# First attention's scores: two f32r products of stacked high and low parts in place of one f32 product

## What is computed

```python
h = h + _L0_attn_ref(_layernorm(h, axis=-1), L0_attn_Wq, L0_attn_bq, L0_attn_Wk, L0_attn_bk, L0_attn_Wv, L0_attn_bv)
...
q = jnp.einsum('bnh,oh->bno', x, Wq) + bq
k = jnp.einsum('bnh,oh->bno', x, Wk) + bk
v = jnp.einsum('bnh,oh->bno', x, Wv) + bv
scores = jnp.einsum('bik,bjk->bij', q, k)
attention = jax.nn.softmax(scores, axis=-1)
attended = jnp.einsum('bij,bjk->bik', attention, v)
```

## Time and profile before

| what | value |
|---|---|
| median of 3 runs | 5632.31 us (5630.87 to 5649.04) |
| the profiled execution | 5644.55 us |
| its span, first to last instruction | 5642.7 us |
| TensorE (PE) busy | 4372.6 us, 77% |
| VectorE busy | 3331.4 us, 59% |
| ScalarE busy | 1815.6 us, 32% |
| GpSimd busy | 425.7 us, 8% |
| TensorE on the chain that ended last | 49% of the span |
| mean granted TensorE clock | 0.822 |

### The profile page before, as it was taken

How to read it: one execution, slowest core, us unless ns; L and a number is a source line. 1 busy time by engine, 2 the same in 40 slices (tenths; PEclk the granted TensorE clock), 3 DMA queues, 4 the chain that set the end, 5 groups by cost and what they waited for, 6 DMA issues and landing times.

```text
span 5642.7 us, 71238 instructions
## 1 busy us (share of the span) xinstructions
PE 4372.6 (77%) x26536; PEld 2924.2 (52%) x26536; DVE 3331.4 (59%) x9075; ACT 1815.6 (32%) x2723; POOL 425.7 (8%) x484
## 2 busy tenths in 40 slices
PE   6886755799888755699888755699887765699987
PEld 4554544555646534555546534555546544555646
DVE  4444769555545669555555669555555659655554
ACT  2232521144332522134332422134332421234432
POOL 0100000011100000011100000021100000011100
PEclk9898865699988975599988975699988975689988
DMA  2000000000000000000000000000000000000000
GB/s 80 3 3 15 1 16 1 1 1 1 1 1 4 1 16 1 1 1 1 1 1 4 1 16 1 1 1 1 1 1 4 1 1 1 1 1 1 1 1 4
DMA packets 28309, 26.48 MB, mean 5 GB/s; under 512 B 10550, under 2 KB 26934, under 8 KB 27450
## 3 DMA queue, kind: packets, MB, share of 16 engines
q1 hardware_dynamic: 27962, 21.98, 1.4%
HBM read 20.40 MB, written 1.57 MB: 4 GB/s over the span
## 4 chain that ended last, share of the span: by engine, by line
PE 49%; DVE 29%; issue 5%; POOL 4%; ACT 3%; DVEq 1%; SPq 0%; POOLq 0%; ACTq 0%
PE ps L581 10%; PE ps L615 7%; DVE qup L759 4%; PE ps L1584 3%; DVE x L757 3%; PE ps L1600 3%; DVE x L761 3%; DVE ctxt L802 3%; PE ps L642 3%; DVE ctxt L798 2%; POOL st L394 2%; PE ps L915 2%; PE ps L414 2%; PE ps L427 2%; DVE row_max L1047 2%
## 5 line engine op out<-in xcount | busy, mean ns | idle before, releaser
L615 PE MATMUL ps<-cst,big 128*128 128x128 f32 x4608 | 674.9, 298 | 345.0 <-ACT big L717 312.5
L615 PEld LDWEIGHTS ps<-cst,big 128*128 128x128 f32 x4608 | 570.1, 154 | 426.3 <-ACT big L717 354.9
L698 ACT COPY big<-ps 128x512 f32<-128x512 f32 x816 | 478.6, 586 | 877.1 <-PE ps L615 877.1
L832 DVE TENSOR_REDUCE negmax<-ps 128x1 f32<-128x1536 f32 x336 | 590.1, 1757 | 64.0 <-PE ps L588 44.8
L717 ACT ACTIVATE big<-ps,negmax 128x1536 f32<-128x1536 f32 x336 | 518.7, 1544 | 269.0 <-DVE negmax L832 269.0
L409 PE MATMUL ps<-cst 128*128 128x512 f32 x608 | 332.5, 707 | 127.4 <-DVEq L187 58.2
L394 POOL TENSOR_TENSOR st<-st,cst 128x6 f32<-128x6 f32 x104 | 156.8, 1508 | 3449.3 <-DVE st L382 3445.2
L581 PE MATMUL ps<-kup,qup 128*128 128x512 f32 (+3 forms) x768 | 358.1, 563 | 41.8 <-POOLq L187 41.0
L588 PE MATMUL ps<-qlo 128*128 128x512 f32 x576 | 343.9, 736 | 7.4 <-DVEq L187 7.4
L422 ACT COPY xt<-ps 64x512 f32<-64x512 f32 x144 | 80.7, 579 | 828.0 <-PE ps L414 828.0
L642 PE MATMUL ps<-big,v 128*32 128x128 f32 (+1 forms) x8064 | 324.7, 278 | 8.1 <-DVE ctxt L1071 6.0
(11 more groups left out here) (317 smaller groups left out, 7131.4 us busy)
## 6 DMA issues: line engine op xcount, KB each, us to landing
rw<-in_w_route SPq DMA_DIRECT2D x128, 64.5 KB, 1.8
cst<-in_consts SPq DMA_DIRECT2D x1, 2671.0 KB, 14.7
cst<-in_consts SPq DMA_DIRECT2D x1, 2670.5 KB, 8.8
big<-in_consts SPq DMA_DIRECT2D x1, 1872.5 KB, 22.0
out_dram<-res SPq DMA_DIRECT2D x4, 384.0 KB, 2.8
experts_in<-in_consts SPq DMA_DIRECT2D x1, 1360.0 KB, 17.5
qup<-in_patches SPq DMA_DIRECT2D x4, 260.0 KB
klo<-in_pe_low SPq DMA_DIRECT2D x2, 384.0 KB, 23.3
```

The lines of the kernel that those rows point to most:

```text
L615: ins = nc.tensor.transpose(turned_bank(kind, u, g)[:, i * P:(i + 1) * P], prob[:, slot_of(kind, u), (4 * g + i) * P:(4 * g + i + 1) * P], ...
L698: copy(pt[:, slot_of(kind, u), g, 0:n], turned_bank(kind, u, g)[:, 0:n]).then_inc(*ph.mark(copier(kind, g)))
L832: nc.vector.tensor_reduce(negmax[:, u:u + 1], flat[:, 0:n], AX.X, ALU.max, negate=True)\
```

## The change

q and k of the first attention are no longer kept in f32. TensorE makes each of them twice, one copy under the other: the weights are repeated by VectorE at the start of each batch (`twice`), and a product has 128 output rows in place of 64. The blocks come as q, k, q, k, q, k. ScalarE writes each block rounded to f32r (the high part) to `q_stack` or `k_stack`. VectorE then subtracts it from the exact block: in the lower half of the rows of q (64 to 127), so that `q_stack` holds the high part above the low part; for k on all 128 rows into a second plane, so that plane 0 of `k_stack` holds the high part twice and plane 1 the low part twice. The scores of a bank are two f32r products with the same stationary `q_stack` tile, added in PSUM: (q high + q low) with k high, then with k low. POOL no longer clears `qlo` in this phase.

```diff
-        def qkv_pe(ph, pe, wq, wk, wv):
+        def qkv_blocks():
+
+            return [(w, j) for j in range(NB) for w in range(2)]
+
+        def qkv_pe(ph, pe):
             keep_clock(1, 9)
             pe.wait_ge(*ph.after("normed", 1))
             transpose_pe(ph, x, [0, 1, 2])
-            for j in range(NB):
+            pe.wait_ge(*ph.after("weights_spread", 2))
+            for i, (w, j) in enumerate(qkv_blocks()):
                 pe.wait_ge(*ph.after("xt_copied", j + 1))
-                nc.tensor.matmul(ps[0:D, 3 + j, :], W(wq), xt[:, 512 * j:512 * (j + 1)], start=True, stop=True)\
-                    .then_inc(*ph.mark("q_psum"))
-            for j in range(NB):
-                nc.tensor.matmul(ps[0:D, (6 + j) % 8, :], W(wk), xt[:, 512 * j:512 * (j + 1)], start=True, stop=True)\
-                    .then_inc(*ph.mark("k_psum"))
-            rows_pe(ph, W(wv), xt, [1, 2], "v_psum")
+                nc.tensor.matmul(ps[:, (3 + i) % 8, :], twice[:, w, :, :].rearrange("p r d -> p (r d)"), xt[:, 512 * j:512 * (j + 1)], start=True, stop=True)\
+                    .then_inc(*ph.mark("stack_psum"))
+            rows_pe(ph, W("v0"), xt, [1, 2], "v_psum")
...
-            for j in range(NB):
-                act.wait_ge(*ph.after("k_psum", j + 1))
-                nc.scalar.copy(kt[0:D, 512 * j:512 * (j + 1)], ps[0:D, (6 + j) % 8, :])
...
+            for i, (w, j) in enumerate(qkv_blocks()):
+                act.wait_ge(*ph.after("stack_psum", i + 1))
+                nc.scalar.activation((q_stack, k_stack)[w][:, 0, 512 * j:512 * (j + 1)].bitcast(F32R), ps[:, (3 + i) % 8, :],
+                                     ACT.Identity).then_inc(*ph.mark("high_ready"))
...
+        def qkv_vec(ph, dve):
+            for i, (w, j) in enumerate(qkv_blocks()):
+                cols = slice(512 * j, 512 * (j + 1))
+                dve.wait_ge(*ph.after("high_ready", i + 1))
+                if w == 0:
+                    ins = nc.vector.scalar_tensor_tensor(q_stack[D:P, 0, cols].bitcast(F32R), ps[D:P, (3 + i) % 8, :], 1.0,
+                                                         q_stack[D:P, 0, cols], ALU.mult, ALU.subtract)
+                else:
+                    ins = nc.vector.scalar_tensor_tensor(k_stack[:, 1, cols].bitcast(F32R), ps[:, (3 + i) % 8, :], 1.0,
+                                                         k_stack[:, 0, cols], ALU.mult, ALU.subtract)
+                ins.then_inc(*ph.mark("low_ready"))
...
+                elif kind == "attn0":
+                    for part in range(2):
+                        ins = nc.tensor.matmul(bank, q_stack[:, 0, qs].bitcast(F32R), k_stack[:, part, lo * P:hi * P].bitcast(F32R),
+                                               start=(part == 0), stop=(part == 1))
...
                 pool.wait_ge(consts_in, CONST_DMAS)
-                clear_upper(ph, pool)
                 norm_pool(ph, pool, 1)
...
+                for w, name in enumerate(("q0", "k0")):
+                    nc.vector.tensor_copy(twice[:, w, :, :], W(name).unsqueeze(1).to_broadcast([P, 2, D]))\
+                        .then_inc(*ph.mark("weights_spread"))
                 dve.wait_ge(patches_in, 32 * (b + 1))
                 nc.vector.tensor_copy(h[:, TP:T, :], txt_in)
```

More of the change, by code:

```diff
@@ L51 @@
 SIGNALS = {
-    "embed": {"pool_step": 1, "rstd_ready": 2, "xt_copied": 3, "emb_psum": 1, "xt_psum": 3, "q_psum": 3, "k_psum": 3,
+    "embed": {"weights_spread": 2, "rstd_ready": 2, "xt_copied": 3, "emb_psum": 1, "xt_psum": 3, "stack_psum": 6, "high_ready": 6, "low_ready": 6,
         "v_psum": 2, "vec_step": 13, "var_ready": 2, "normed": 1},
@@ L277, in build @@
         work = qup[:, 0, :]
+        twice = big[:, 0:2 * P].rearrange("p (w r d) -> p w r d", w=2, r=2)
         spread = big[:, 0:4 * P].rearrange("p (w h r d) -> p w h r d", w=2, h=2, r=4)
@@ L455, in qkv_vec @@
-        def qkv_vec(ph, dve, scale):
-            for j in range(NB):
-                dve.wait_ge(*ph.after("q_psum", j + 1))
-                nc.vector.tensor_scalar(qt[0:D, 512 * j:512 * (j + 1)], ps[0:D, 3 + j, :], scale, None, ALU.mult)
+            for i, (w, j) in enumerate(qkv_blocks()):
+                act.wait_ge(*ph.after("stack_psum", i + 1))
+                nc.scalar.activation((q_stack, k_stack)[w][:, 0, 512 * j:512 * (j + 1)].bitcast(F32R), ps[:, (3 + i) % 8, :],
+                                     ACT.Identity).then_inc(*ph.mark("high_ready"))
@@ L1370, in _ @@
                 ins.then_inc(*ph.mark("emb_psum"))
-                qkv_pe(ph, pe, "q0", "k0", "v0")
+                qkv_pe(ph, pe)
                 ph.leave(pe)
@@ L1652, in _ @@
                 ready_vec(ph, dve)
-                qkv_vec(ph, dve, 1.0)
+                qkv_vec(ph, dve)
                 ph.leave(dve)
```

## The result

| | before | after |
|---|---|---|
| median, measured side by side | 5632.31 us (5630.04 to 5654.71, 5 runs) | 5593.23 us (5590.42 to 5602.71, 5 runs) |
| ratio, 95% interval | | 0.9921 [0.9898, 0.9944] |
| profiled execution | 5644.55 us | 5591.80 us |
| its span | 5642.7 us | 5589.9 us |
| TensorE busy | 4372.6 us | 4269.8 us |

The change saves 39 us, 0.8%. The forecast was 5586. In the view of lines the 576 records of the earlier trace rows have come apart: 288 stay f32, the third layer's, and 288 are f32r, with a line of their own, the first attention's.

The account below looks back on a forecast made before the run. TensorE, busy without a gap, bounds first attention's units. Shorter score records save 1.16 + 0.28 + 10.4 = 11.9 us a batch, 47.4 in four, less 0.2: 5586 us forecast, range 5568 to 5605.

Parts of the forecast that it names:

- Spacing and unit: First attention's scores: f32r records 0.236 us apart instead of 0.430, so a unit falls from 5.77 to 4.61 us.
- Rival 4: First attention's score products cost their columns alone, 0.215 us a record, giving 5580 us; chance 0.06.
- rival 2: Score records sharing weights and bank don't overlap: at 0.50 us each, unit 6.2 us, total 5649 us; chance 0.05.
- Start of the stage: First attention's start: first maximum gains 1.16 us; second turn comes 3.74 us after the first, gaining 0.28.
- Rival 1: Clock falls at each first-attention start, TensorE idle 2.2 us; costs 2.4 us a batch, total 5595 us; chance 0.12.
- it is a good deal shorter than 3.65, and 1.08 did no harm: Argument against a clock fall at first attention's start: idle 2.2 us, against 3.65 in layer 1's attention and 1.08 before.
- The other chains: In a first-attention unit the softmax chain has 0.87 us to spare and VectorE's queue 0.18 us.
- rival 3: VectorE's queue (copy, strips, scaling, maximum) takes over the first-attention unit, at 5.1 us; total 5602 us; chance 0.05.
- Projections: Ahead of first attention: doubled output rows cost nothing; the last subtraction hides behind value products with 0.15 us to spare.
- Clearing and weight copies: Batch start: the dropped POOL clearing gains nothing, two weight copies of 0.25 us fit; batch one loses 0.2 us.
- The sum: First attention gains 11.9 us a batch, 47.4 us in four; less 0.2 us lost in batch one, 47 us.
- The route, expert and later attention stages where they were: Stages behind the first pass stay as they were, changing by no more than a few us.

Follow-up runs that it names:

- one and three products: Changed kernel, slow way never taken, with one or three f32r products per score bank in place of two: 5538.53 us and 5584.54 us.
- f32 stacks: Changed kernel, slow way never taken, with one f32 product per bank of stacked q and the high part of k: 5611.03 us, ratio 0.9958.
- before, never: Kernel before, with the third layer's test raised to 2.0 so that its full search is never taken: 5640.99 us, ratio 1.0004.
- six memsets: Six one-column memsets added to VectorE's set-up, slow way never taken: 5609.58 us in the kernel before, 5576.79 us in the changed kernel.

## Why the prediction was right, and where it was not

The time came out as forecast, 5593 for 5586, inside the range. Its mechanism held in the first pass. That the total agreed was partly luck: two things that it had not foreseen nearly cancel. Without the first of them, the slow way, the kernel takes 5562.82 us, below the range of 5568 to 5605.

- **Spacing and unit: right.** 0.236 us a record and 4.61 us a unit were forecast; 0.236 (the median) and 4.58 were measured, TensorE busy throughout at clock 1.00. The runs with one and three products give 0.23 and 0.24. Rival 4 (0.215) is out by the same rows, and so is rival 2. The estimate of 216 ns from the Trainium skill's "TensorE: Matmul & The Clock Gate" (Back-to-back issue gap) does not agree with them either.
- **Start of the stage: right, except for the clock.** The maximum gained 1.18 (forecast 1.16), and the second turn follows in 3.74 where the clock stays. Rival 1, put at 0.12, came in two batches of four, and in 5 of 16 over all traces with this gap. The step "it is a good deal shorter than 3.65, and 1.08 did no harm" was too sure: 2.28 us of idle time can be enough. Its price of 2.4 a batch was too high: the second turn came 1.29 and 1.10 us late, and filling the gap gave back 1.3 and 1.2 us in the stage.
- **The other chains: right.** VectorE's queue had 0.16 us to spare (forecast 0.18), so rival 3 stayed away.
- **Projections: right.** The f32 stacks have the first pass of before. The 0.15 us ahead of the first value copy was gone: it starts right behind the last subtraction, without an idle time (middle row). The second one waits for TensorE's value products, as the prediction said it would:

```profile
272.88 0.69 DVE L467 SCALAR_TENSOR_TENSOR k_stack<-ps,k_stack 128x512 fp32r<-128x512 f32 x1 [0.16 <-ACT k_stack L456]
273.54 0.56 DVE L472 COPY v<-ps 128x384 f32<-128x384 f32 x1
274.88 0.56 DVE L472 COPY v<-ps 128x384 f32<-128x384 f32 x1 [0.78 <-PE ps L428]
```

- **Clearing and weight copies: right.** They are worth nothing in a batch. In the set-up 0.2 us was gained instead of lost (the first normalisation ends at 61.59 instead of 61.77).
- **The sum: 47.4 forecast for the first pass, 49.7 measured.** By the unit and the start a batch gains 9 x 1.19 + 1.18 + 0.28 = 12.2. Batches three and four gained 13.4, one and two, with the fallen clock, 11.8 and 11.1. In the former the wait ahead of the projections was shorter as well, since the clock stood higher while TensorE ran its idle products. From the normalised input to the first score it was 300.01 - 288.21 = 11.80 us before and 275.52 - 265.17 = 10.35 after. It need not be the change's doing, since kernels with f32 scores vary as much there: before, never, has 10.50 us in batch two and 11.55 in batch three, the f32 stacks 10.38 and 10.85. No run was made on it.
- **"The route, expert and later attention stages where they were": wrong.** This step failed twice, and by the prediction's own last sign (no change of more than a few us behind the first pass) that part of the forecast was wrong. One tile in the third layer took the slow way (+30 us), most likely because last bits changed. And the later passes became some 20 us faster (39.1 + 30.4 - 49.7 by the medians, 21.4 in the fourth layer by the profile). The kernels with six memsets show that a shift of VectorE's instructions alone can do as much: 27 us in before. How the 20 of this change divide between the 21st unit and the clock at the stage's start was not settled. 50 - 30 + 20 is the 39 measured, to 1 us. By design the change gives the 50; the 30 hang on these inputs, and the 20 on placement and clock.

## What to carry to other kernels

Where TensorE is busy without a gap, count its records and take their spacing from a stage that already has the form; that gave the unit within 0.03 us here. Then read which parts of the program have a path that depends on data or on the clock: one tile on the slow way cost 30 us, and in before six more instructions moved 27, each more than half of what the change itself gives. Before crediting or blaming an edit for less than 1%, compare like stretches of the two traces stage by stage, and run a kernel with the same number of instructions that does nothing.

## What the runs showed of the hardware

- **VectorE pauses at a place of its list.** About 0.35 us, without a row of its own, in all four batches of a kernel at the same instruction: in the fourth layer's attention ahead of the scaling of the 11th unit in before and its variants without memsets at the front, ahead of the masked copy of the 21st in after, its variants without memsets, and before with six memsets. Six instructions elsewhere in the list move it. What it is stays open.
- **Clock.** 2.3 us of idle time behind 3.0 us of products let the granted clock fall in 5 batches of 16, 2.96 us in 3 of 4; 1.6 us and less did in none of 32. In the tail of a stage, a shift of 0.35 us decided whether TensorE's same 2564 records cost 350.7 or 356.9 us, where the clock had been at 0.50 for the stage's first 12.6 to 13.1 us.
- **A copy beside a memset.** VectorE's two weight copies took 2.57 us beside POOL's memset and 0.36 without it.
